# A decoder layer on one core: selective-scan states of two blocks summed on TensorE, the end of softplus on VectorE, feed-forward scales folded into the weights

## The chip, the cores and the metric

The kernel runs on 1 core of one Trainium2 chip. The metric is the device time of one execution in microseconds (us), and the time before is the median of 3 runs. The engines are named PE (TensorE), DVE (VectorE), ACT (ScalarE), POOL (GpSimd) and SP (SyncE, which only issues DMAs here).

## What is computed

One layer over 16 sequences of 64 tokens with 128 features, all in f32: a selective-scan (Mamba) block, a cross-attention without softmax, and a gated feed-forward part, each followed by a layer norm of the sum with its input.

```python
xz = x @ W_in_o + b_in_o
x_proj, z_proj = xz[..., :256], xz[..., 256:]
xm, zm = split(x_proj @ W_in_i)                       # 256 and 256
xc = silu(causal_depthwise_conv(xm, conv_w, conv_b))  # 4 taps
dt, Bm, Cm = split(xc @ W_xp)                         # 128, 16, 16
delta = softplus(dt @ W_dt + b_dt)
h = exp(delta * A) * h + (delta * xc) * Bm            # step by step along the sequence, 16 states per channel
y = sum over states of h * Cm, + D_skip * xc
out = ((y * silu(zm)) @ W_out_i * sigmoid(z_proj)) @ W_out_o + b_out_o
x = layernorm(x + out)
q, k, v = heads of (x, ctx, ctx)                      # 16 heads of 8, q and k of unit length
x = layernorm(x + ((q k^T) ** 2 @ v) @ Wo^T + bo)
h = silu(x @ w1^T * s1) * (x @ w2^T * s2)             # 512 hidden
h = gelu(h @ h1^T * h1s); h = gelu(h @ h2^T * h2s)    # erf gelu
x = layernorm(x + h @ w3^T * s3)
```

## The kernel before

Everything is kept transposed, features on the 128 partitions and tokens along the free axis. The 1024 tokens are cut into 4 blocks of T = 256 (4 sequences). For each block five strands of work are interleaved by hand: front (`xm`, `delta`, `bc`, `soft`, `soft_end`), gates, keys and values, attention with the Mamba output (`mamba_y`, `gate_out`, `proj_out`, then `query`, `attend`, `attn_out`), and feed-forward (`gate_up`, `hid1`, `hid2`, `down`). The table `ORDER` lists for each engine, word by word, in which order it works; the words are executed in that order, so a step that waits holds everything behind it on its engine. `gate_up:1:3` is part 3 of the step for block 1; `scan:9` is scan step 9 of 32.

The scan. The 256 channels are two halves (`CH`), and the 16 states go in 8 steps per block of 2 states (`SG`) each, so one step handles 2 x 2 x 256 = 1024 columns, and the four blocks have 32 steps. A step is four operations on three engines:

- ACT writes the decay exp(delta A) to PSUM (`decay_`, L767, four of 252 columns; `DA_RING` = 2 steps).
- POOL writes the input delta xc B to `state` (`scan_in`, L1054). B and C come broadcast over the partitions through DRAM (`b_fetch`, `c_fetch`, three buffers each).
- DVE runs the recurrence in place (`scan`, L937).
- POOL multiplies the state in place by C (`scan_out`, L1063).

`state` holds two groups of four steps. When the four products of a group are there, DVE sums its 8 states with one reduction (`reduce`, L944) that reads them 512 elements apart, into `part`. PE adds the two parts and D_skip xc (`mamba_y`, L545 and L547), DVE gates the sum (`mamba_y`, L973), PE and DVE go on with `gate_out` (L557, L981).

Softplus (`delta`, `soft`, `soft_end`) is max(p,0) + log(1+exp(-|p|)) with a correction of the rounding: ACT takes Abs (L740), Exp into PSUM (L748) and Ln into SBUF (L752); then DVE takes `trunc` (L918), `rest` (L924) and their sum with the logarithm (L926, its two tensors both in SBUF). The end, delta = pre + rest and du = delta xc (`soft_end_of`, L332 and L336, both inputs in SBUF), is on DVE for block 0 and on POOL for blocks 1 to 3; `scan_in` of the block waits for it. POOL also makes the masked queries (`mask_queries`, L344) for blocks 0 to 2.

The feed-forward part takes the ternary weights as they are. `gate_up` has 4 parts of 128 hidden features: PE (L631), Tanh with the scale on ACT (L834), two operations on DVE (L1023, L1026). `hid1` and `hid2` have 4 parts each: 4 matmuls (L641) and a Gelu of 256 columns with the scale (L842). A layer norm is Square (L790, L786), a matmul with 1/128 (L573), Ln and Exp (L796, L801) and one DVE operation (L1001, L992). ACT's functions need a table to be loaded where they change (L672).

PE's results go through four PSUM banks of 512 columns that are handed out in the order of the list, so a step waits until the fourth result before it has been read. An f32 matmul leaves two matmul records in the trace.

## Time and profile before

| | |
|---|---|
| median of 3 runs (lowest, highest) | 270.6 us (268.74, 270.67) |
| the profiled execution, its own time | 269.1 us |
| its span, first to last instruction | 267.3 us |
| mean granted clock of TensorE | 0.874 of 2.4 GHz |
| busy: PE, DVE, ACT, POOL | 206.5, 184.4, 179.0, 165.4 us |
| table loads on ACT | 41, 52.6 us |

The span is 1.8 us shorter than the execution's own time, and that is 1.5 us under the median. A busy figure is a sum over the whole span; which engine ends a stage is read from the stretches and from what waits. Times within the span are given from its start.

### The profile page before, as it was taken

The page shows a single profiled execution, that of the slowest core. Times are in us where ns is not written, and L with a number is a line of the kernel's source. Part 1 is how long each engine was busy: PE and PEld are TensorE (multiplying, and loading weights), DVE is VectorE, ACT ScalarE, POOL GpSimd, SP SyncE. Part 2 cuts the span into 40 slices and gives each one's busy share as a digit, 9 for nine tenths or more (in the row PEclk, how much of TensorE's full clock was granted, in tenths as well). Part 3 has the DMA queues.
Part 4 walks back from the last instruction along what each step waited for, and adds up shares of the span by engine and source line. Part 5 has one row for each costly group of instructions (what it writes and reads, how often), then busy time and mean ns, then how long its engine had stood idle before and what let it go on. Part 6 is the DMA issues. An engine that isn't in the chain of part 4 may idle for free.

```text
span 267.3 us, 3857 instructions
## 1 busy us (share of the span) xinstructions
PE 206.5 (77%) x1426; PEld 154.3 (58%) x1426; DVE 184.4 (69%) x159; ACT 179.0 (67%) x340; POOL 165.4 (62%) x80
## 2 busy tenths in 40 slices
PE   8996291039585566899949809999999999999992
PEld 6674071017263244686637405777777788778881
DVE  0226619999989998998999998897996452105000
ACT  4055973744898376798976934679966967775523
POOL 4000999999999999999999599599930000000000
PEclk9999777557799555999999855999999999999998
DMA  6986620267105304222046013200000000000000
GB/s 216 422 370 236 237 83 1 78 198 273 75 5 207 114 12 147 81 78 82 0 159 238 2 49 108 81 0 20 4 0 4 20 0 2 2 0 2 21 0 20
DMA packets 6980, 24.38 MB, mean 91 GB/s; under 512 B 945, under 2 KB 1714, under 8 KB 6834
## 3 DMA queue, kind: packets, MB, share of 16 engines
q1 hardware_dynamic: 6962, 24.14, 25.7%
q8 instruction: 11, 0.18, 0.3%
q14 instruction: 7, 0.06, 0.1%
HBM read 23.48 MB, written 0.66 MB: 90 GB/s over the span
## 4 chain that ended last, share of the span: by engine, by line
PE 38%; POOL 22%; DVE 15%; issue 12%; ACT 9%; DMA 2%; SPq 0%; DVEq 0%; ACTq 0%; POOLq 0%
PE work L641 15%; POOL state L1054 11%; POOL state L1063 10%; DVE part L944 10%; PE work L631 4%; ACT L672 3%; DMA cw_row<-cw 2%; PE work L651 2%; DVE state L937 2%; PE work L613 2%; PE work L458 1%; PE work L597 1%; PE work L545 1%; PE work L557 1%; PE work L487 1%
## 5 line engine op out<-in xcount | busy, mean ns | idle before, releaser
L1054 POOL TENSOR_TENSOR state<-du,b_buf 128x1024 f32<-128x1024 f32 x32 | 75.6, 2386 | 26.3 <-DVE du L336 22.9
L1063 POOL TENSOR_TENSOR state<-state,c_buf 128x1024 f32<-128x1024 f32 x32 | 74.7, 2361 | 3.4 <-DVE state L937 3.4
L937 DVE TENSOR_TENSOR_SCAN state<-decay,state 128x1024 f32<-128x1024 f32 x32 | 71.7, 2273 | 5.5 <-ACT decay L767 3.5
L767 ACT ACTIVATE decay<-delta,neg_a 128x252 f32<-128x252 f32 x128 | 52.4, 462 | 19.0 <-DVE state L937 12.4
L944 DVE TENSOR_REDUCE part<-state 128x512 f32<-128x4096 f32 x8 | 58.2, 7289 | 0.2
L672 ACT ACT_TABLE_LOAD x41 | 52.6, 1283 | 1.4 <-PEq L1126 0.7
L641 PE MATMUL work<-hid_b,mat 128*128 128x256 f32 x128 | 29.9, 383 | 0.6 <-ACT zgate L734 0.6
L641 PE MATMUL work<-hid_a,mat 128*128 128x256 f32 x128 | 29.4, 382 | 0.1
L641 PEld LDWEIGHTS work<-hid_b,mat 128*128 128x128 f32 x128 | 23.9, 190 | 5.3 <-ACT zgate L734 1.0
L641 PEld LDWEIGHTS work<-hid_a,mat 128*128 128x128 f32 x128 | 23.9, 190 | 4.5 <-DVE hid_a L1026 0.5
L631 PE MATMUL work<-x,mat 128*128 128x256 f32 x64 | 17.0, 419 | 2.3 <-issue 1.7
L545 PE MATMUL work<-part,mat 128*128 128x512 f32 x16 | 11.0, 825 | 9.3 <-DVE part L944 6.4
L631 PEld LDWEIGHTS work<-x,mat 128*128 128x128 f32 x64 | 12.9, 210 | 6.6 <-issue 4.7
L992 DVE TENSOR_TENSOR final<-work,root_ffn 128x256 f32<-128x256 f32 x4 | 1.7, 418 | 21.8 <-ACT root_ffn L801 21.8
L471 PE MATMUL work<-x,wfz 128*128 128x256 f32 x16 | 5.4, 466 | 14.4 <-DVE vmask L965 13.6
L458 PE MATMUL work<-x,wf 128*128 128x256 f32 (+3 forms) x64 | 15.4, 383 | 0.1
L842 ACT ACTIVATE hid_c<-work,vec 128x256 f32<-128x256 f32 x16 | 7.3, 472 | 10.0 <-PE work L641 9.9
L458 PEld LDWEIGHTS work<-x,wf 128*128 128x128 f32 x64 | 11.7, 191 | 1.8 <-DMA x<-xT 0.5
L471 PEld LDWEIGHTS work<-x,wfz 128*128 128x128 f32 x16 | 3.3, 223 | 15.4 <-DVE vmask L965 13.8
L545 PEld LDWEIGHTS work<-part,mat 128*128 128x128 f32 x16 | 3.8, 256 | 13.2 <-issue 10.1
L1001 DVE SCALAR_TENSOR_TENSOR x<-work,b_centred,root_attn 128x256 f32<-128x256 f32 x8 | 3.8, 480 | 10.7 <-ACT root_attn L801 10.6
L834 ACT ACTIVATE up<-work,half_s 128x256 f32<-128x256 f32 x16 | 7.4, 474 | 5.1 <-PE work L631 3.0
(132 smaller groups left out, 333.5 us busy)
## 6 DMA issues: line engine op xcount, KB each, us to landing
b_buf<-bc_scratch SPq DMA_DIRECT2D x16, 512.0 KB, 3.9
c_buf<-bc_scratch SPq DMA_DIRECT2D x16, 512.0 KB, 4.3
mat<-mats SPq DMA_DIRECT2D x1, 2560.0 KB, 14.6
mat<-mats SPq DMA_DIRECT2D x1, 640.0 KB, 3.9
cw_row<-cw SPq DMA_DIRECT2D x1, 512.0 KB, 6.1
x<-xT SPq DMA_DIRECT2D x1, 512.0 KB, 7.0
kv<-ctxT SPq DMA_DIRECT2D x1, 512.0 KB, 8.9
outT<-final SPq DMA_DIRECT2D x4, 128.0 KB, 1.7
```

The lines of the kernel that those rows point to most:

```text
L458: mm(o[:, :, late:], wf4[:, k, c * P:(c + 1) * P], xs[:, :, 0:SEQ - late], start=(late == 0), stop=False, skip_group_check=True)
L471: i = mm(tile(("zm", b))[:, c * T:(c + 1) * T], wfz[:, c * P:(c + 1) * P], x[:, tok(b)], start=True, stop=True)
L545: mm(o[:, :], ident, part[(GROUPS * b + g) % 2][:, :], start=(g == 0), stop=False, skip_group_check=True)
L631: i = mm(tile(("gu", b, j))[:, n * T:(n + 1) * T], m(w)[:, j * P:(j + 1) * P], x2[b % 2][:, :], start=True, stop=True)
L641: i = mm(tile((key, b, j))[:, 0:T], w[:, k, j * P:(j + 1) * P], src[:, k, :], start=(k == 0), stop=(k == FT - 1))
L672: nc.scalar.preload_act_table_set(name)
L767: i = act_(decay[:, s % DA_RING, k, c, :].rearrange("p (s t) -> p s t", t=SEQ)[:, :, 1:], delta[b % KEEP][:, c, :].rearrange("p (s t) -> p ...
L834: act_(up[j % 2][:, :], tile(("gu", b, j))[:, 0:T], ACT.Tanh, scale=half_s1[:, j:j + 1]).then_inc(up_ready, 1)
L937: vec_.tensor_tensor_scan(h, decay[:, s % DA_RING, :, :, :].rearrange("p k c t -> p (k c t)"), h, 0.0, ALU.mult, ALU.add).then_inc(scanned, 1)
L944: vec_.tensor_reduce(part[g % 2][:, :], state[g % 2][:, :, :, :, :].rearrange("p q k c t -> p (c t) (q k)"), axis=AX.X, op=ALU.add).then_i ...
L1054: nc.gpsimd.tensor_tensor(slot(s), du[b % KEEP][:, None, :, :].broadcast_to([P, SG, CH, T]), b_buf[c % B_RING][:, states, None, :].broadca ...
L1063: nc.gpsimd.tensor_tensor(slot(s), slot(s), c_buf[c % C_RING][:, states, None, :].broadcast_to([P, SG, CH, T]), ALU.mult).then_inc(product, 1)
```

## The change

1. **States.** `state` becomes a ring of 4 steps, and `scan_out` writes its products to a tensor of their own, `prod`. For blocks 0 and 1 PE sums them with the identity into the block's bank, two 512-column matmuls for each step as its product comes (`mamba_sum`, L653 of the changed kernel), and the skip term behind them. For blocks 2 and 3 POOL writes `prod` with the two states of a step side by side, and DVE sums in three reductions: 4 steps, then 3 steps with the first result and the skip term (made by ACT, `skip`), then the last step with the second result; the sum stays in SBUF and DVE gates it from there.
2. **Softplus and masks.** `soft_end` and `mask_queries` are on DVE for all blocks. Exp stays in SBUF, `trunc` and `rest` read it there, and Ln goes to PSUM, beside them. For block 0 the table of Exp and Ln is loaded ahead of `delta`.
3. **Feed-forward.** DVE multiplies the scales into the weights once (`fold`, four operations), and `gate_up`, `hid1` and `hid2` have 2 parts of 512 columns each.
4. **Loads and buffers.** B and C have two buffers each. The weights of the output projection, of the queries and of the feed-forward part are loaded behind the first `bc_store` and, the last 2560 KB, behind `b_fetch:4`, with 1024 KB of broadcast scales. A step that opens a PSUM bank takes the one longest free. Ln and Exp of the norms share a buffer; the bias of the values is one matmul.
5. **Order.** All five lists are written anew.

```diff
-GROUP = 4
-GROUPS = STEPS // GROUP
+GROUP_OF = (0, 0, 0, 0, 1, 1, 1, 2)
+GROUPS = 3
+SLOT_OF = (0, 1, 2, 3, 4, 5, 6, 0)
+SUMMED = (slice(0, 4), slice(4, 8), slice(0, 9, 8))
+EXTRA = (7, 8)
+SLOTS = 9
+SUM_ON = ("pe", "pe", "dve", "dve")
+SOFT_END_ON = ("dve", "dve", "dve", "dve")
+MASK_ON = ("dve", "dve", "dve", "dve")
+OUT_ON_DVE = ()
 TAPS = 4
 HEADS, DK = 16, 8
 HG, HI = 4, 4
...
-B_RING, C_RING = 3, 3
+B_RING, C_RING = 2, 2
+RING = 4
 WARM_UP = 18
-KEEP = 2
+KEEP, XC_KEEP = 2, 3
...
     "dve": """
-        prep prep2 bc:0 delta:0 soft:0 soft_end:0 key_norm:0 scan:0 scan:1 bc:1 delta:1 soft:1 scan:2 scan:3 scan:4
...
+        prep bc:0 delta:0 soft:0 soft_end:0 scan:0 scan:1 scan:2 bc:1 scan:3 prep3 delta:1 soft:1 prep2 scan:4
+        scan:5 soft_end:1 bc:2 delta:2 soft:2 scan:6 scan:7 scan:8 scan:9 key_norm:0 soft_end:2 centre_b fold:0
...
-        state = [sb(f"state{i}", [GROUP, SG, CH, T]) for i in range(2)]
-        part = [sb(f"part{i}", [CH * T]) for i in range(2)]
+        state = [sb(f"state{i}", [SG, CH, T]) for i in range(RING)]
+        prod = sb("prod", [SLOTS, CH, T, SG])
...
-        hid_a, hid_b, hid_c = (sb(n, [FT, T]) for n in ("hid_a", "hid_b", "hid_c"))
+        pre, expo, rest, yg = (sb(n, [CH, T]) for n in ("pre", "expo", "rest", "yg"))
+        hid_a, hid_b = (sb(n, [FT, T]) for n in ("hid_a", "hid_b"))
+        hid_c = hid_a
...
+        def wait_slot_read(eng, s):
+
+            b, n = divmod(s, STEPS)
+            if SUM_ON[b] == "pe":
+                eng.wait_ge(summed, summed_by_pe(s) + 1)
+            else:
+                eng.wait_ge(reduced, reduces_of(b) + GROUP_OF[n] + 1)
...
+        def products(b, n):
+
+            if SUM_ON[b] == "pe":
+                return prod[:, SLOT_OF[n], :, :, :].rearrange("p c t k -> p (c t k)").rearrange("p (k c t) -> p k c t", k=SG, c=CH)
+            return prod[:, SLOT_OF[n], :, :, :].rearrange("p c t k -> p k c t")
...
+        def out_product(eng, engine, s, done):
+
+            c = s // CHUNK
+            b, n = divmod(s, STEPS)
+            slots = [k for k in range(s) if SLOT_OF[k % STEPS] == SLOT_OF[n]]
+            if slots:
+                wait_slot_read(eng, slots[-1])
+            eng.wait_ge(scanned, s + 1)
+            eng.wait_ge(c_loaded[c % C_RING], 16 * (c // C_RING + 1))
+            states = slice(s % CHUNK * SG, (s % CHUNK + 1) * SG)
+            engine.tensor_tensor(products(b, n), slot(s),
+                                 c_buf[c % C_RING][:, states, None, :].broadcast_to([P, SG, CH, T]), ALU.mult).then_inc(done, 1)
...
+            def late(n):
+                if n == 0:
+                    load_mats(4)
+                    load_mats(5)
+                    return
+                load_mats(6)
+                for i, h in enumerate((hid_a, hid_b)):
+                    two = slice(i * 2 * HID, (i + 1) * 2 * HID)
+                    sp.dma_start(h[:, :, :].rearrange("p k t -> p (k t)"), srow[:, two].broadcast_to([P, 2 * HID])).then_inc(loaded["srow"], 16)
...
+            def mamba_sum(s):
+                b, n = divmod(s, STEPS)
+                if SUM_ON[b] == "dve":
+                    return
+                if n == 0:
+                    pe.wait_ge(diag_ready, 1)
+                    wait_bank_free(pe, ("y", b))
+                wait_products(pe, s + 1)
+                for k in range(SG):
+                    i = mm(tile(("y", b))[:, :], ident, products(b, n)[:, k, :, :].rearrange("p c t -> p (c t)"), start=(n == 0 and k == 0),
+                           stop=False, skip_group_check=True)
+                i.then_inc(summed, 1)
...
+                for key, w in (("g", "w1T"), ("u", "w2T")):
+                    wait_bank_free(pe, (key, b, j))
+                    for n in range(2):
+                        i = mm(tile((key, b, j))[:, n * T:(n + 1) * T], m(w)[:, (2 * j + n) * P:(2 * j + n + 1) * P], x2[b % 2][:, :],
+                               start=True, stop=True)
+                    i.then_inc(filled, 1)
...
+                if b == 0:
+                    exp_ln()
...
-                act.wait_ge(soft_dve, b + 1)
-                e = tile(("dl", b))[:, :]
-                act_(e, expo[:, :, :].rearrange("p c t -> p (c t)"), ACT.Exp, scale=-1.0).then_inc(soft_act, 1)
-                if b > 0:
-                    act.wait_ge(soft_rest, 2 * b)
+                act_(expo[:, :, :], expo[:, :, :], ACT.Exp, scale=-1.0).then_inc(soft_act, 1)
                 act.wait_ge(soft_act, 3 * b + 2)
-                act_(logt[:, :, :].rearrange("p c t -> p (c t)"), e, ACT.Ln, bias=1.0).then_inc(soft_act, 1)
+                act.wait_ge(soft_max, b + 1)
...
+            def skip(b):
+
+                if SUM_ON[b] == "pe":
+                    return
+                wait_emptied(act, ("xm", b))
+                if reduces_of(b) > 0:
+                    act.wait_ge(reduced, reduces_of(b) - GROUPS + 2)
+                for c in range(CH):
+                    i = act_(prod[:, EXTRA[0], c, :, 1], xc[b % XC_KEEP][:, c, :], ACT.Copy, scale=v("d_skip")[:, c:c + 1])
+                i.then_inc(skip_ready, 1)
...
+                act_(up[j][:, :, :].rearrange("p n t -> p (n t)"), tile(("g", b, j))[:, :], ACT.Tanh).then_inc(up_ready, 1)
...
-                    act_(dst[:, j, :], tile((key, b, j))[:, 0:T], ACT.Gelu, scale=v(scale)[:, j:j + 1]).then_inc(used["act"], 1)
+                    act_(dst[:, 2 * j:2 * j + 2, :].rearrange("p n t -> p (n t)"), tile((key, b, j))[:, :], ACT.Gelu).then_inc(used["act"], 1)
...
+            def fold(n):
+                dve.wait_ge(loaded["srow"], 32)
+                dve.wait_ge(loaded["w1T"], 16)
+                if n == 0:
+                    vec_.scalar_tensor_tensor(out=m("w1T"), in0=m("w1T"), scalar=0.5, in1=s_row[0], op0=ALU.mult, op1=ALU.mult).then_inc(folded, 1)
+                    vec_.tensor_tensor(m("w2T"), m("w2T"), s_row[1], ALU.mult).then_inc(folded, 1)
+                    return
+                w = m(f"h{n}T").rearrange("p (k n) -> p k n", k=FT)
+                vec_.tensor_tensor(w, w, s_row[n + 1][:, None, :].broadcast_to([P, FT, HID]), ALU.mult).then_inc(folded, 1)
...
             def soft(b):
-                dve.wait_ge(soft_act, 3 * b + 3)
-                e = tile(("dl", b))[:, :].rearrange("p (c t) -> p c t", c=CH)
-                vec_.tensor_scalar(trunc[:, :, :], e, 1.0, -1.0, ALU.add, ALU.add).then_inc(soft_rest, 1)
+                if b > 0:
+                    dve.wait_ge(soft_step, 2 * b - 1)
+                dve.wait_ge(soft_act, 3 * b + 2)
+                vec_.tensor_scalar(rest[:, :, :], expo[:, :, :], 1.0, -1.0, ALU.add, ALU.add).then_inc(soft_rest, 1)
+                dve.wait_ge(soft_rest, 2 * b + 1)
+                vec_.tensor_tensor(rest[:, :, :], expo[:, :, :], rest[:, :, :], ALU.subtract).then_inc(soft_rest, 1)
                 if b == 0:
                     dve.wait_ge(log_one_ready, 1)
-                else:
-                    dve.wait_ge(soft_step, 2 * b - 1)
-                dve.wait_ge(soft_rest, 2 * b + 1)
-                vec_.tensor_tensor(rest[:, :, :], e, trunc[:, :, :], ALU.subtract).then_inc(used["dve"], 1)
-                wait_emptied(dve, ("dl", b))
-                vec_.scalar_tensor_tensor(out=rest[:, :, :], in0=logt[:, :, :], scalar=log_one[:, 0:1], in1=rest[:, :, :],
-                                          op0=ALU.subtract, op1=ALU.add).then_inc(soft_rest, 1)
+                dve.wait_ge(soft_act, 3 * b + 3)
+                dve.wait_ge(soft_rest, 2 * b + 2)
+                log = tile(("dl", b))[:, :].rearrange("p (c t) -> p c t", c=CH)
+                vec_.scalar_tensor_tensor(out=rest[:, :, :], in0=log, scalar=log_one[:, 0:1], in1=rest[:, :, :],
+                                          op0=ALU.subtract, op1=ALU.add).then_inc(used["dve"], 1)
 
             def soft_end(b):
-                if b == 0:
+                if SOFT_END_ON[b] == "dve":
...
-                vec_.tensor_reduce(part[g % 2][:, :], state[g % 2][:, :, :, :, :].rearrange("p q k c t -> p (c t) (q k)"),
-                                   axis=AX.X, op=ALU.add).then_inc(reduced, 1)
+                src = prod[:, SUMMED[n], :, :, :].rearrange("p q c t k -> p (c t) q k")
+                dst = prod[:, EXTRA[n], :, :, 0].rearrange("p c t -> p (c t)") if n < GROUPS - 1 else part
+                vec_.tensor_reduce(dst, src, axis=AX.XY, op=ALU.add).then_inc(reduced, 1)
...
+                dve.wait_ge(reduced, reduces_of(b + 1))
+                vec_.tensor_tensor(yg[:, :, :], part.rearrange("p (c t) -> p c t", c=CH), mgate[b % KEEP][:, :, :],
+                                   ALU.mult).then_inc(y_ready, 1)
...
+                h = hid_a[:, 2 * j:2 * j + 2, :].rearrange("p n t -> p (n t)")
+                dve.wait_ge(up_ready, b * FP + j + 1)
                 if b > 0 and j == 0:
-                    wait_filled(dve, ("h1", b - 1, FT - 1))
-                vec_.scalar_tensor_tensor(out=h, in0=up[j % 2][:, :], scalar=1.0, in1=ps[:, 0:T], op0=ALU.add,
-                                          op1=ALU.mult).then_inc(up_gated, 1)
-                dve.wait_ge(up_gated, n + 1)
-                vec_.scalar_tensor_tensor(out=h, in0=ps[:, T:2 * T], scalar=half_s12[:, j:j + 1], in1=h, op0=ALU.mult,
-                                          op1=ALU.mult).then_inc(used["dve"], 1)
...
+                vec_.scalar_tensor_tensor(out=h, in0=up[j][:, :, :].rearrange("p n t -> p (n t)"), scalar=1.0, in1=tile(("g", b, j))[:, :],
+                                          op0=ALU.add, op1=ALU.mult).then_inc(used["dve"], 1)
+                wait_emptied(dve, ("g", b, j))
+                wait_filled(dve, ("u", b, j))
+                vec_.tensor_tensor(h, tile(("u", b, j))[:, :], h, ALU.mult).then_inc(used["dve"], 1)
```

What the new lists do to the instructions is shown at three places. First DVE, around the start of block 1's scans. Before, `L937` is the scan, `L926` the last of the softplus sums, `L944` the reduction, `L973` and `L981` the gates:

```order
L937 SCALAR_TENSOR_TENSOR state<-decay,state 128x1024 x2
L904 COPY bc_row<-work 32x256
L911 TENSOR_SCALAR pre<-work,vec 128x256 x2
L918 TENSOR_SCALAR trunc<-work 128x512
L924 TENSOR_TENSOR rest<-work,trunc 128x512
L926 SCALAR_TENSOR_TENSOR rest<-logt,log_one,rest 128x512
L937 SCALAR_TENSOR_TENSOR state<-decay,state 128x1024 x6
L965 TENSOR_TENSOR vmask<-work,rk 128x16x8 x2
L944 TENSOR_REDUCE part<-state 128x512 x2
L937 SCALAR_TENSOR_TENSOR state<-decay,state 128x1024 x2
L973 TENSOR_TENSOR yg<-work,mgate 128x512
```

Now, at the same place, `L1091` is the scan, `L406` and `L410` are the end of softplus for block 2, and `L1043`, `L1044` and `L1047` are three of the four folds:

```order
L1091 SCALAR_TENSOR_TENSOR state<-decay,state 128x1024 x4
L1116 TENSOR_SCALAR ssk<-work 128x32
L1119 RECIPROCAL rk<-ssk 128x32
L406 TENSOR_TENSOR delta<-pre,rest 128x512
L410 TENSOR_TENSOR du<-delta,xc 128x512
L1051 COPY b_centred<-work 128x2
L1043 SCALAR_TENSOR_TENSOR mat<-mat,hid_a 128x512
L1044 TENSOR_TENSOR mat<-mat,hid_a 128x512
L1091 SCALAR_TENSOR_TENSOR state<-decay,state 128x1024
L1141 TENSOR_TENSOR yg<-work,mgate 128x512
L1047 TENSOR_TENSOR mat<-mat,hid_b 128x2048
L1155 SCALAR_TENSOR_TENSOR mat<-zgate,work 128x512
```

Two reductions are gone from between the scans of blocks 0 and 1, and five operations with two inputs in SBUF stand there.

Second POOL, at the passage from block 0 to block 1. Before, `L1054` is `scan_in`, `L1063` is `scan_out`, and `L332`, `L336` end the softplus of block 1:

```order
L1054 TENSOR_TENSOR state<-du,b_buf 128x1024 x5
L1063 TENSOR_TENSOR state<-state,c_buf 128x1024 x7
L332 TENSOR_TENSOR delta<-pre,rest 128x512
L336 TENSOR_TENSOR du<-delta,xc 128x512
L1054 TENSOR_TENSOR state<-du,b_buf 128x1024 x4
L1063 TENSOR_TENSOR state<-state,c_buf 128x1024
```

Now `L1228` is `scan_in` and `L429` is `scan_out`:

```order
L1228 TENSOR_TENSOR state<-du,b_buf 128x1024 x2
L429 TENSOR_TENSOR prod<-state,c_buf 128x1024 x4
L1228 TENSOR_TENSOR state<-du,b_buf 128x1024 x4
L429 TENSOR_TENSOR prod<-state,c_buf 128x1024 x2
L1228 TENSOR_TENSOR state<-du,b_buf 128x1024
L429 TENSOR_TENSOR prod<-state,c_buf 128x1024
```

POOL has nothing but the two kinds of scan steps, and it takes them closer together.

Third PE, at the output of block 0. Before, `L545` adds the two parts, `L547` the skip term, and `L557` is `gate_out`:

```order
L471 MATMUL work<-x,wfz 128x256 x2
L478 MATMUL work<-x,mat 128x256 x4
L458 MATMUL work<-x,wf 128x256
...
L545 MATMUL work<-part,mat 128x512 x2
L547 MATMUL work<-xc,diag_d 128x256 x2
L515 MATMUL work<-vec,mat 128x2
L557 MATMUL work<-yg,mat 128x256 x4
```

Now `L653` is the sum of the states (here of steps 5 to 7), `L659` the skip term, `L670` is `gate_out`:

```order
L631 MATMUL work<-mat,k 128x16 x2
L653 MATMUL work<-prod,mat 128x512 x6
L659 MATMUL work<-xc,mat 128x256 x2
L576 MATMUL work<-x,wfz 128x256 x4
L583 MATMUL work<-x,mat 128x256 x4
L670 MATMUL work<-yg,mat 128x256 x4
```

The sum hangs on POOL's product directly, with no step of DVE between.

## Rows read from the trace of the kernel before

**Rows 1.** Stretches of the span: length, busy time (and instructions) by engine, granted clock, DMA.

```profile
core 0: us, PE busy (x) PEld busy (x) DVE busy (x) ACT busy (x) POOL busy (x), PEclk, DMA share, GB/s
0.00:26.20 26.20, 23.41 (x112) 17.45 (x112) 8.23 (x24) 9.59 (x17) 2.75 (x8) 1.00 0.81 310
26.20:145.50 119.30, 75.02 (x419) 52.91 (x420) 107.59 (x69) 87.28 (x176) 118.74 (x53) 0.79 0.35 118
145.50:160.60 15.10, 7.48 (x53) 4.59 (x52) 15.10 (x5) 10.53 (x22) 11.98 (x8) 0.73 0.10 25
160.60:210.30 49.70, 48.89 (x466) 36.62 (x467) 41.29 (x37) 37.44 (x72) 31.96 (x14) 0.95 0.09 31
210.30:267.30 57.00, 51.74 (x379) 42.74 (x378) 12.24 (x28) 34.20 (x57) 0.00 (x0) 0.98 0.02 6
```

**Rows 2.** The chain that ended last, around the first scan step: start, us, what.

```profile
13.62 0.98 PE work L437 x8
...
16.55 0.63 PE work L520 x2
...
19.80 0.94 ACT L672
...
21.73 0.60 ACT logt L752
...
26.17 2.35 POOL state L1054
```

**Rows 3.** Groups by line: busy us, mean ns of one, idle time before and its releasers.

```profile
L1054 POOL TENSOR_TENSOR state<-du,b_buf 128x1024 f32<-128x1024 f32 x32 | 75.6, 2386 | 26.3 <-DVE du L336 22.9 <-DVE part L944 3.3
L937 DVE TENSOR_TENSOR_SCAN state<-decay,state 128x1024 f32<-128x1024 f32 x32 | 71.7, 2273 | 5.5 <-ACT decay L767 3.5 <-POOL state L1054 2.0
L944 DVE TENSOR_REDUCE part<-state 128x512 f32<-128x4096 f32 x8 | 58.2, 7289 | 0.2
L672 ACT ACT_TABLE_LOAD x41 | 52.6, 1283 | 1.4 <-PEq L1126 0.7
L834 ACT ACTIVATE up<-work,half_s 128x256 f32<-128x256 f32 x16 | 7.4, 474 | 5.1 <-PE work L631 3.0 <-DVE hid_a L1023 2.1
L344 POOL TENSOR_TENSOR qmask<-q,vec 128x1024 f32<-128x1024 f32 x3 | 6.0, 2016 | 0.2 <-ACT q L807 0.2
L336 POOL TENSOR_TENSOR du<-delta,xc 128x512 f32<-128x512 f32 x3 | 3.8, 1280 | 0.2
L748 ACT ACTIVATE work<-expo 128x512 f32<-128x512 f32 x4 | 2.4, 596 | 1.8 <-DVE pre L911 1.8
L344 DVE TENSOR_TENSOR qmask<-q,vec 128x1024 f32<-128x1024 f32 x1 | 1.2, 1226 | 3.0 <-ACT q L807 3.0
L336 DVE TENSOR_TENSOR du<-delta,xc 128x512 f32<-128x512 f32 x1 | 0.7, 693 | 0.0
```

**Rows 4.** DVE in order of time: start, us, engine, line; the four times of L926.

```profile
23.88 0.75 DVE L926 SCALAR_TENSOR_TENSOR rest<-logt,log_one,rest 128x512 f32<-128x512 f32 x1
...
41.65 1.26 DVE L926 SCALAR_TENSOR_TENSOR rest<-logt,log_one,rest 128x512 f32<-128x512 f32 x1
...
89.82 1.98 DVE L926 SCALAR_TENSOR_TENSOR rest<-logt,log_one,rest 128x512 f32<-128x512 f32 x1
...
139.57 6.55 DVE L926 SCALAR_TENSOR_TENSOR rest<-logt,log_one,rest 128x512 f32<-128x512 f32 x1
```

**Rows 5.** POOL in order of time, beside the waits of rows 4 and steady.

```profile
42.32 2.79 POOL L1054 TENSOR_TENSOR state<-du,b_buf 128x1024 f32<-128x1024 f32 x1
...
91.22 2.81 POOL L1054 TENSOR_TENSOR state<-du,b_buf 128x1024 f32<-128x1024 f32 x1
...
133.96 11.62 POOL L1063 TENSOR_TENSOR state<-state,c_buf 128x1024 f32<-128x1024 f32 x5
```

**Rows 6.** PE in order of time: `gate_out:3`, and the sixteen matmuls of `hid2:3`.

```profile
210.33 1.89 PE L557 MATMUL work<-yg,mat 128*128 128x256 f32 x8
...
252.74 7.07 PE L641 MATMUL work<-hid_b,mat 128*128 128x256 f32 x32
```

403 lines of the change are left out of this document (233 added, 170 removed).

## The prediction

> **What bounds the kernel now.** I read the stretches first [rows 1], cut where the scan phase changes hands: from POOL's first scan step (26.2 us) to the last product of block 2 (145.5), from there to the moment PE can take that block's output (160.6), from there to `gate_out` of block 3 (210.3), and the tail. In the first, POOL is busy 118.7 of 119.3 us and DVE 107.6: the scan runs at POOL's pace, with DVE 90% full beside it. In the second DVE is busy all the time (two reductions) and PE half. In the third and fourth PE is busy 48.9 of 49.7 and 51.7 of 57.0, at a clock near 2.4 GHz; POOL works 32 of the 49.7 us and not at all after them, so it does not decide there. So the end is the sum of four things: POOL's start, POOL's 48 operations for blocks 0 to 2 with what it does between, 15 us of reductions, and 107 us of PE.
>
> The chain at the start [rows 2] shows what precedes POOL: the bias matmuls of `prep2` (0.98 us), the keys of block 0 (0.63), a table load that shows for 0.94, Ln (0.60). The groups [rows 3] give prices. Last, L926, the one DVE operation that reads two tensors in SBUF while POOL works: 0.75 us with POOL idle, and 1.26, 1.98 and 6.55 with POOL busy [rows 4]. In the first two cases DVE got in where one POOL operation followed another, and that next one took 2.79 and 2.81 us instead of the 2.32 of its neighbours (11.62 for five) [rows 5]. In the third it was passed over at two such places. So these operations exclude POOL's, and the wait is a POOL operation's remainder or more.
>
> The Trainium skill, page "SBUF — State Buffer", section "Who interferes with whom", says why: a VectorE operation with two SBUF inputs takes the port pair that GpSimd reads through, whole instructions at a time. Rows 4 agree, and add that the lock can be lost twice running.
>
> **Start.** Removed from the chain are the four pieces of rows 2, 0.98 + 0.63 + 0.94 + 0.60 = 3.2 us (Ln now lies beside `trunc` and `rest`; the table is loaded under the delta matmuls). POOL starts at 23.0. `b_fetch:0` now has 768 KB of weights ahead of it on SP's queue but the 2560 KB no longer; I take it as landed, and 2 us late as the bound.
>
> **POOL.** The 64 scan operations stay, at a pitch of 2.32 [rows 5]: 48 take 111.4 us, 16 take 37.1. Three ends of softplus (2 x 1.28 each) and three masks (2.02) go [rows 3], 13.7 us. Products into a tensor of their own, from block 2 with a step of 8 bytes in the output, are not in the trace; the bounds are no change (input and output in place take the same 2.3 us) and 10% on 16 products, 4 us. I take no change.
>
> **The port.** What leaves POOL comes to DVE with two SBUF inputs, and the change adds more of these: for blocks 1 to 3 the subtraction in `soft` (3) and `soft_end` (6), masks 0 to 2 (3), the folds (4), the gate of block 2 (1): 17 while POOL works, where there were 3. L926 itself now reads PSUM and leaves the list. A wait was 0.5, 1.2 and 5.8 us (rows 4 less 0.75), median 1.2, mean 2.5. I take 1.9, between them: 32 us on DVE. POOL loses 0.45 for each short one [rows 5], about 1.0 for a mask and 2 for a large fold, 12 us in all. So POOL gains 13.7 and pays 12: alone it would bring block 2's last product at 23.0 + 111.4 + 11 = 145.4, as before.
>
> By the same page (section "Who interferes with whom") also single-source f32 operations from SBUF to SBUF contend; that would be `trunc` of blocks 1 to 3 and three small ones, six more waits, some 11 us by 1.9 each. No row shows such an operation beside POOL, so the sum leaves it out.
>
> **DVE up to block 2's gate.** In the first stretch DVE was busy 107.6 us [rows 1]. Four reductions go (4 x 7.3 = 29.2), and L926 with its waits (1.26 + 1.98 + 5.9 of the last one = 9.2); 69.2 stay, 24 scans at 2.2 [rows 3] among them. To these come L926 at its bare 0.75 three times (2.3); the ends of softplus, 6 x 0.69 (4.2); two masks (2.5); the folds, 0.7 + 0.7 + 2.3 + 2.3 (512 elements take 0.69 and 1024 take 1.23 [rows 3], 1.05 ns for an element more); gate, values and diagonal that now fall here (2.0); and three reductions. 4096 elements read 512 apart cost 7.29 us [rows 3], 1.78 ns each. Now two neighbours lie together. Bounds: 4.4 us as if contiguous, 7.3 as before. I take 5.0, nearer the contiguous row since half of the jumps go, and 2.6 for the short one, 12.6 together. The pairs in `gate_up` save 0.8. Sum: 69.2 + 2.3 + 4.2 + 2.5 + 6.0 + 2.0 + 12.6 - 0.8 = 98.0. DVE stood 11.7 us in that stretch [rows 1], for decays and POOL; I keep half, 5.5. It starts at 25.3, one POOL operation after 23.0. With 15 waits of 1.9 (28.5) block 2 is gated at 25.3 + 98.0 + 5.5 + 28.5 = 157.3. POOL would allow 145.4 + 2.6 + 0.7 = 148.7: DVE is the bound.
>
> The page's section "Door 1: The DMA port swizzle" says that two accesses to one 16-byte line hide the jump. Then the reductions cost 4.4, and the sum falls by 2 us; the trace has no row of it.
>
> **DVE to block 3's gate.** 8 scans (17.6), reductions 5.0 + 5.0 + 2.6, `gate_up` 2.8, mask 1.2, the rest 4.5, one wait 1.9: 40.6. `gate_out:3` can start at 197.9. POOL's 16 operations from 145.4 end by 185, and PE's work from `gate_out:2` to `gate_out:3` is 72 matmuls of 256 columns at 0.43 (16 in 6.9 us [rows 6]) and 3.5 us of attention, 34.5: 157.3 + 34.5 = 192. Neither decides, each has 6 us or more of room.
>
> **What is hidden.** The state sums add 32 matmuls of 512 columns (27.8 us) and take away eight and four short ones, 19 us net, in the stretch where PE was busy 75 of 119 at 0.79 of the clock. They are short and each step's two follow a product; at 1.2 GHz they take 3.5 us per 4.7 us of POOL's time. Cover gone, block 1's attention is late and `gate_out:2` with it: up to 5 us. POOL needs a sum only when it comes round to the slot (after the eighth step). ACT loses ten table loads (41 to 31, 12.8 us) and about 8 us by 512-column functions (0.60 against 2 x 0.47); it had 32 us free in that stretch, so nothing shows. The 3.6 MB behind `b_fetch:4` stand before `c_fetch:3`: at most 4 us, once, taken as 0.
>
> **Tail.** After `gate_out:3` the same 57.0 us of work stand [rows 1, 6], with one norm matmul more (0.4). The paired parts cost in front of `hid1:3`: Tanh and Gelu of 512 columns are 0.12 later each, and hid1 starts when two DVE operations of 0.69 instead of 0.45 are done; `down:2` is now ahead of the last `gate_up` and no longer covers it. By these rows PE stands 1.1 us more. 57.0 + 0.4 + 1.1 = 58.5.
>
> **Sum.** 197.9 + 58.5 = 256.4 is the span, and 1.8 more the own time: 258.2. The profiled execution is 1.5 under the median of the runs, so the forecast is 259.7, taken as 260.0 (3.9% less than 270.6).
>
> **Rivals.**
> - *DVE gets in at every boundary.* For it: two of three rows. Each wait is then 1.2 or less, DVE gains 16 x 0.7 = 11, and POOL decides: last product at 185, the two last reductions and the gate done at 191, and 58.5 + 3.3: 253. If the port costs POOL nothing either, PE is next: 148.7 + 34.5 + 58.5 + 3.3 = 245. Chance 0.20.
> - *Reductions as slow as before.* 2.3 us more on each of four and 1.1 on two, all on DVE's path: 11 more, 271. For it: nothing in the trace shows a faster one. Chance 0.12.
> - *The port takes what POOL gave.* The mean wait is that of the rows, 2.5, or the single-source ones wait too (the page's rule above): 17 x 0.6 or 11 us more, 270. Against it: a POOL that waits for scans leaves the port free. Chance 0.12.
> - *Slower.* The wait of row 139.57 is the rule where POOL has a row of ready products: 5.8 for 1.9. Its place is the subtraction and the two ends of softplus, on which `scan_in` of the next block waits. Each costs 3.9; four of them make the change worth nothing beyond 273, six give 283. Chance 0.11.
> - *Forecast*, DVE bound with some of each: 254 to 267. Chance 0.45.
>
> A measurement of this kernel can tell about 1% from no change: under 267.9 is faster, over 273.3 slower. Faster: 0.45 + 0.20 and a fifth of the two cases at 270, 0.70. Slower: 0.11 and an eighth of those two, 0.14. The rest, 0.16, is within 1%. The range, 246 to 274, runs from PE as the bound to the two cases at 270 with their upper edge, and leaves out the slow rival.
>
> **What would show it.** Right: the two-input DVE operations (L406, L410, L437, L1074, the folds) at a mean of 2 to 3 us each where POOL is busy; POOL idle 10 us or more for scans; the reduction near 5 us; POOL's first step at 23; the table group at 31; PE's sums never ahead of POOL in what a wait names; 58 us from `gate_out:3` to the end. Wrong: POOL without idle time (then the first rival), L1108 at 7 us (the second), any single L406 or L410 over 5 us again and again (the fourth), or PE as what DVE and POOL wait for.

## The result and the profile after

The changed kernel takes 262.26 us (median of 4 runs, 261.55 to 264.52) against 269.67 of the kernel before beside it: ratio 0.974, 95% interval 0.969 to 0.979. The forecast was 260.0 us, a ratio of 0.961 against its 270.6. So 2.6% was gained where 3.9% was forecast. In the profiled execution the span fell from 267.3 to 260.4 us, 6.9 less, and the own time is 262.3.

| Point in the span | before | forecast | after |
|---|---|---|---|
| first scan step on POOL | 26.2 | 23.0 | 23.0 |
| gate of block 2 begins (before: its sum can be taken) | 160.6 | 156.6 | 155.9 |
| gate of block 2 done | | 157.3 | 156.8 |
| last product on POOL done | 196.1 | about 185 | 192.9 |
| `gate_out:3` begins on PE | 210.3 | 197.9 | 199.6 |
| from there to the end | 57.0 | 58.5 | 60.8 |
| span | 267.3 | 256.4 | 260.4 |

The stretches of the span after the change, cut where the forecast cut them (stretch and length, then busy time and count by engine, granted clock, DMA share), against [rows 1]:

```profile
core 0: us, PE busy (x) PEld busy (x) DVE busy (x) ACT busy (x) POOL busy (x), PEclk, DMA share, GB/s
23.00:156.00 133.00, 108.02 (x539) 68.93 (x538) 121.89 (x84) 89.38 (x185) 124.21 (x50) 0.88 0.37 131
156.00:199.60 43.60, 40.12 (x445) 31.34 (x443) 40.12 (x33) 36.76 (x69) 33.27 (x15) 1.00 0.17 53
199.60:260.40 60.80, 53.41 (x379) 42.02 (x378) 10.68 (x20) 24.86 (x41) 0.00 (x0) 0.98 0.02 8
```

Up to block 2's gate DVE is busy 121.9 of 133.0 us and POOL 124.2: neither is full, and each stands for the other at times. PE has 108 us there, where before it had 75 of 119, at a granted clock of 0.88 instead of 0.79. The stretch of 15 us that two reductions on DVE filled from end to end [rows 1] is gone.

The groups of DVE between 20 and 215 us (busy us, mean ns of one, idle before and who ended it), where the forecast had its prices:

```profile
L1091 DVE TENSOR_TENSOR_SCAN state<-decay,state 128x1024 f32<-128x1024 f32 x32 | 72.1, 2276 | 6.4 <-POOL state L1228 4.5 <-ACT decay L897 1.9
L1108 DVE TENSOR_REDUCE prod<-prod 128x512 f32<-128x4096 f32 x4 | 17.6, 4412 | 2.0 <-POOL prod L429 2.0
L437 DVE TENSOR_TENSOR qmask<-q,vec 128x1024 f32<-128x1024 f32 x4 | 13.3, 3334 | 0.0
L1074 DVE TENSOR_TENSOR rest<-expo,rest 128x512 f32<-128x512 f32 x3 | 8.2, 2722 | 0.1
L410 DVE TENSOR_TENSOR du<-delta,xc 128x512 f32<-128x512 f32 x4 | 6.8, 1708 | 0.1
L406 DVE TENSOR_TENSOR delta<-pre,rest 128x512 f32<-128x512 f32 x4 | 6.2, 1560 | 0.0
L1047 DVE TENSOR_TENSOR mat<-mat,hid_b 128x2048 f32<-128x2048 f32 x2 | 5.3, 2636 | 0.0
L1108 DVE TENSOR_REDUCE mat<-prod 128x512 f32<-128x2048 f32 x2 | 4.6, 2281 | 0.1
L1072 DVE TENSOR_SCALAR rest<-expo 128x512 f32<-128x512 f32 x3 | 4.5, 1497 | 0.0
```

The scan costs what it did (2273 ns [rows 3]). A reduction of 4096 elements takes 4.41 us where 7.29 was the price of before [rows 3]. The masks (L437) average 3.33 us against a bare 1.23 [rows 3], the subtraction (L1074) 2.72. `trunc` (L1072), one input and one output in SBUF, took 0.42 us while POOL had not begun and 1.5 on average of the three beside it. The first two of its rows:

```profile
18.51 0.42 DVE L1072 TENSOR_SCALAR rest<-expo 128x512 f32<-128x512 f32 x1
...
39.97 1.79 DVE L1072 TENSOR_SCALAR rest<-expo 128x512 f32<-128x512 f32 x1
```

POOL in order of time: the rows that have a wait of 1 us or more in front of them.

```profile
23.00 9.28 POOL L1228 TENSOR_TENSOR state<-du,b_buf 128x1024 f32<-128x1024 f32 x4 [19.74 <-DMA b_buf<-bc_scratch]
49.09 5.11 POOL L429 TENSOR_TENSOR prod<-state,c_buf 128x1024 f32<-128x1024 f32 x2 [2.36 <-DVE state L1091]
...
74.44 2.35 POOL L429 TENSOR_TENSOR prod<-state,c_buf 128x1024 f32<-128x1024 f32 x1 [3.02 <-PE work L653]
...
149.25 2.38 POOL L429 TENSOR_TENSOR prod<-state,c_buf 128x1024 f32<-128x1024 f32 x1 [3.42 <-issue]
...
188.21 4.69 POOL L429 TENSOR_TENSOR prod<-state,c_buf 128x1024 f32<-128x1024 f32 x2 [3.41 <-DVE state L1091]
```

The four stalls behind the first row, with one of 0.21 us that is not shown, are the 12.4 us that POOL loses between 23 and 193. The second is a wait for PE: step 8's product goes where step 0 and step 7 lay, and their sum came late. The one at 149 us, for which the profile names nobody, ends as DVE finishes the scan that stood behind a mask of 5.30 us.

### The profile page after: what moved, and what is told of

Same layout as the page of the kernel before. It is cut to its first block, busy times and chain, and to the rows that moved or that the text cites. A ratio compares the mean times of both kernels' runs of the same rounds, so it can differ in the third digit from the quotient of the medians.

```text
span 260.4 us, 3882 instructions
## 1 busy us (share of the span) xinstructions
PE 223.2 (86%) x1458; PEld 158.4 (61%) x1458; DVE 180.0 (69%) x153; ACT 160.3 (62%) x310; POOL 160.2 (62%) x71
## 4 chain that ended last, share of the span: by engine, by line
PE 33%; DVE 22%; issue 17%; POOL 14%; ACT 7%; DMA 5%; SPq 0%; DVEq 0%; POOLq 0%; ACTq 0%
PE work L760 13%; DVE state L1091 8%; POOL prod L429 7%; POOL state L1228 7%; PE work L563 4%; ACT L792 3%; DVE qmask L437 3%; DMA b_buf<-bc_scratch 2%; DVE rest L1074 2%; DMA cw_row<-cw 2%; PE work L653 2%; DVE prod L1108 2%; PE work L710 2%; PE work L686 2%; PE work L670 1%
## 5 line engine op out<-in xcount | busy, mean ns | idle before, releaser
L1228 POOL TENSOR_TENSOR state<-du,b_buf 128x1024 f32<-128x1024 f32 x32 | 82.1, 2586 | 19.7 <-DMA b_buf<-bc_scratch 19.7
L429 POOL TENSOR_TENSOR prod<-state,c_buf 128x1024 f32<-128x1024 f32 x32 | 76.4, 2407 | 12.4 <-DVE state L1091 6.0
L1091 DVE TENSOR_TENSOR_SCAN state<-decay,state 128x1024 f32<-128x1024 f32 x32 | 72.1, 2276 | 6.4 <-POOL state L1228 4.5
L653 PE MATMUL work<-prod,mat 128*128 128x512 f32 x64 | 35.0, 691 | 10.3 <-DVE mat L1032 7.8
L792 ACT ACT_TABLE_LOAD x31 | 39.8, 1283 | 1.3 <-PEq L1296 0.7
L653 PEld LDWEIGHTS work<-prod,mat 128*128 128x128 f32 x64 | 13.5, 220 | 25.5 <-issue 12.3
L1108 DVE TENSOR_REDUCE prod<-prod 128x512 f32<-128x4096 f32 x4 | 17.6, 4412 | 2.0 <-POOL prod L429 2.0
L563 PE MATMUL work<-x,wf 128*128 128x256 f32 (+3 forms) x64 | 17.9, 428 | 0.2 <-DVE bf L1015 0.2
L984 ACT ACTIVATE hid_a<-work 128x512 f32<-128x512 f32 x8 | 4.8, 597 | 14.5 <-PE work L760 14.5
L437 DVE TENSOR_TENSOR qmask<-q,vec 128x1024 f32<-128x1024 f32 x4 | 13.3, 3334 | 0.0
L710 PE MATMUL work<-qmask,keys 32*64 32x256 f32 x128 | 8.8, 389 | 3.5 <-DVE qmask L437 2.4
L984 ACT ACTIVATE hid_b<-work 128x512 f32<-128x512 f32 x8 | 4.8, 596 | 11.4 <-PE work L760 11.4
## 6 DMA issues: line engine op xcount, KB each, us to landing
mat<-mats SPq DMA_DIRECT2D x1, 2560.0 KB, 10.5
```

The source lines that it names most:

```text
L429: engine.tensor_tensor(products(b, n), slot(s), c_buf[c % C_RING][:, states, None, :].broadcast_to([P, SG, CH, T]), ALU.mult).then_inc(don ...
L437: engine.tensor_tensor(qmask[:, :, :], q[:, None, :].broadcast_to([P, HI, T]), v("hmask")[:, :, None].broadcast_to([P, HI, T]), ALU.mult). ...
L563: mm(o[:, :, late:], wf4[:, k, c * P:(c + 1) * P], xs[:, :, 0:SEQ - late], start=(late == 0), stop=False, skip_group_check=True)
L653: i = mm(tile(("y", b))[:, :], ident, products(b, n)[:, k, :, :].rearrange("p c t -> p (c t)"), start=(n == 0 and k == 0), stop=False, ski ...
L710: i = mm(tile(("s", b, g))[e * SEQ:(e + 1) * SEQ, p * HI * SEQ:(p + 1) * HI * SEQ], keysT[b % KEEP][r, t:t + SEQ], qmask[r, :, t:t + SEQ], ...
L792: nc.scalar.preload_act_table_set(name)
```

## The experiments

Ratios are to the kernel before, run beside it on the same chip; "gate 2" and "gate 3" are the starts of `mamba_y:2` and `mamba_y:3` on DVE in the profiled execution. The first column of times is the span of that execution. The executions of one kernel lie 1 to 4.2 us apart, and not all rows come from one chip. So a difference of spans or gates is one pair of executions, and it is the ratios that decide.

| Kernel | span | gate 2 | gate 3 | median us | ratio (95%) |
|---|---|---|---|---|---|
| changed kernel | 260.4 | 155.9 | 197.7 | 262.26 | 0.974 (0.969 to 0.979) |
| e1 reductions read 512 apart | 272.1 | 161.6 | 208.0 | 272.98 | 1.013 (1.008 to 1.018) |
| e2 masks from PSUM | 257.5 | 151.6 | 194.8 | 258.81 | 0.960 (0.954 to 0.966) |
| e3 end of softplus on POOL, late | 273.2 | 168.8 | 210.6 | 274.57 | 1.018 (1.011 to 1.024) |
| e4 no folding | 256.5 | 150.6 | 193.9 | 257.74 | 0.951 (0.943 to 0.958) |
| e5 block 2 summed on PE | 267.6 | 160.4 | 205.0 | 269.64 | 1.001 (0.999 to 1.004) |
| e6 all sums on DVE | 279.9 | 174.0 | 217.2 | 281.69 | 1.045 (1.039 to 1.051) |
| e7 end of softplus on POOL, early | 265.9 | 160.0 | 203.2 | 267.05 | 0.989 (0.983 to 0.996) |
| e8 the end | 259.5 | 155.3 | 198.5 | 261.99 | 0.970 (0.964 to 0.977) |
| e9 three moves of order | 267.3 | 159.9 | 204.7 | 267.58 | 0.987 (0.981 to 0.993) |
| e10 e2, e8 and e9 | 260.8 | 159.0 | 199.8 | 262.38 | 0.970 (0.964 to 0.976) |
| e11 e10, sums 14 and 15 ahead | 262.6 | 159.0 | 201.6 | 265.32 | 0.980 (0.975 to 0.985) |
| e12 e2 and e8 | 255.1 | 152.1 | 194.1 | 255.94 | 0.947 (0.940 to 0.953) |

The theory at the start was that of the forecast: DVE sets the pace up to block 3's gate, slowed by waits for a port that it shares with POOL. The rival was that POOL, or PE with its sums, is as near to the path as DVE.

**e1: the layout of the products.** The two states of a step 512 elements apart again.

```diff
-            if SUM_ON[b] == "pe":
-                return prod[:, SLOT_OF[n], :, :, :].rearrange("p c t k -> p (c t k)").rearrange("p (k c t) -> p k c t", k=SG, c=CH)
-            return prod[:, SLOT_OF[n], :, :, :].rearrange("p c t k -> p k c t")
+            return prod[:, SLOT_OF[n], :, :, :].rearrange("p c t k -> p (c t k)").rearrange("p (k c t) -> p k c t", k=SG, c=CH)
...
-                src = prod[:, SUMMED[n], :, :, :].rearrange("p q c t k -> p (c t) q k")
+                src = prod[:, SUMMED[n], :, :, :].rearrange("p q c t k -> p q (c t k)").rearrange("p q (k n) -> p n q k", k=SG)
```

> One part undone: POOL writes the products of blocks 2 and 3 as it does those of blocks 0 and 1, the two states of a step 512 elements apart, and the three reductions of each block read them 512 apart. Theory A (VectorE sets the pace up to the gate of block 3, and the neighbours of 8 bytes are what makes a reduction cheap): the 4096-element reductions take 7.3 us again instead of 4.4 and the 2048-element ones 3.6 instead of 2.3, 2 x (2.9 + 2.9 + 1.3) = 14 us more on VectorE, all on the path: 276 us, slower than the kernel before. Rival B (VectorE has slack before both gates, since it also waits for GpSimd and TensorE there): half of that is hidden, 269 us. Rival C (the layout is not what counts, the reductions in three pieces are): 4.4 us stay and the time is 262 us.

The one line of the reduction in this kernel (count, then shortest, median and longest in ns, first and last start):

```profile
L1109 DVE TENSOR_REDUCE prod<-prod x4: 7204/7325/7397, 134.7 to 196.6; 128x512 f32<-128x4096 f32 x4
L1109 DVE TENSOR_REDUCE mat<-prod x2: 3699/3745/3791, 157.6 to 204.2; 128x512 f32<-128x2048 f32 x2
```

A reduction costs 1.8 ns an element when its two neighbours are 512 apart and 1.08 when they lie together. Six reductions are 14.6 us longer in sum, gate 3 is 10.3 later and the span 11.7 longer: 0.7 of the added time counts at the gate and 0.8 in the span, between A and B and nearer to A, and C is out. The 1.4 us between the two lie behind gate 3, where the edit changes nothing; why was not looked for. With this one part undone the kernel is 1.3% slower than before. The other side of the layout cost nothing: POOL's undisturbed products take 2.35 us in both kernels, with a step of 8 bytes in the output or without.

**e2: one SBUF operand less in the masks.**

```diff
-            engine.tensor_tensor(qmask[:, :, :], q[:, None, :].broadcast_to([P, HI, T]), v("hmask")[:, :, None].broadcast_to([P, HI, T]),
-                                 ALU.mult).then_inc(qm_ready, 1)
+            engine.scalar_tensor_tensor(out=qmask[:, :, :], in0=tile(("q", b))[:, None, 0:T].broadcast_to([P, HI, T]), scalar=v("bq"),
+                                        in1=v("hmask")[:, :, None].broadcast_to([P, HI, T]), op0=ALU.add, op1=ALU.mult).then_inc(used["dve"], 1)
...
-                act_(q[:, :], tile(("q", b))[:, 0:T], ACT.Identity, bias=v("bq")).then_inc(q_ready, 1)
```

> One cost taken away: the masked queries are made from PSUM, (q + bias) x mask in one VectorE operation with one large SBUF operand less, and ScalarE's copy of q falls away. Theory A (port): masks 0, 1 and 2 take 1.2 us each beside a busy GpSimd instead of 3.4, 5.3 and 3.4; VectorE gains 8.4 us before the gate of block 3 and the time falls by 7 to 8 us, to 254 us. Rival B (VectorE is not alone on the path; GpSimd's own stalls and TensorE's queue take over): masks 1.2 us but a gain of only 2 to 4 us, 259 us. Rival C (the long durations are a wait for something else than the SBUF port): masks stay at 3 us or more and the time at 262 us.

The group of the masks in this kernel, and that of the two large folds:

```profile
L1044 DVE TENSOR_TENSOR mat<-mat,hid_b 128x2048 f32<-128x2048 f32 x2 | 6.8, 3416 | 0.0
...
L437 DVE SCALAR_TENSOR_TENSOR qmask<-work,vec 128x1024 f32<-128x1024 f32 x4 | 5.1, 1271 | 0.0
```

The masks cost 1.27 us whether POOL works or not, so the long durations hung on where the input lies: C is out. The masks save 8.2 us, the span falls by 2.9 and the median by 3.5, which is B's range. Part of the rest is seen in the first row: others wait more, the large folds at 3.42 instead of 2.64 us, and one of the small ones at 2.84 instead of 0.68. In sum the two-input operations other than the masks wait 3.8 us more than in the changed kernel.

**e3 and e7: the end of softplus back on POOL.** e3 has it late in POOL's list, e7 where DVE's list has it.

```diff
-SOFT_END_ON = ("dve", "dve", "dve", "dve")
+SOFT_END_ON = ("dve", "pool", "pool", "pool")
```

> One part undone: the end of softplus of blocks 1 to 3 is on GpSimd again, ahead of steps 8, 15 and 22 of scan_in. VectorE loses six operations that took 11.7 us with their waits, GpSimd gets 3 x 2 x 1.28 = 7.7 us. Theory A (VectorE alone sets the pace): about 10 us less, 252 us. Rival B (GpSimd has 12 us of idle time before its last product and about as much stretched operations, so what it takes over is paid from there and the trade is even): 260 to 264 us. Rival C (what GpSimd gave up was the gain of the change): slower, 268 us or more.

What DVE waited for in e3 (us in total, times, the longest), the row of interest:

```profile
DVE pre L1065 <- POOL delta L407: 20.4, 2, 12.3
```

DVE stood 12.3 us in one piece: `delta:3` on DVE may overwrite `pre` only when POOL has read it, and POOL came to that step only at 102 us. So e3 measured a bad place in the list and says nothing on the trade, though its time falls under C.

> The end of softplus of blocks 1 to 3 on GpSimd as in e3, but at the places in its list that answer to those of VectorE's list: ahead of steps 6, 10 and 18 of scan_in. In e3 VectorE stood 12.3 us in one piece for the end of block 2's softplus, which came late in GpSimd's list. Theory A (that wait was all that made e3 slow; the trade itself is even, since what GpSimd gets, 7.7 us, is about 0.65 of the 11.7 us that VectorE loses): 260 to 264 us. Rival B (GpSimd's time is dearer than VectorE's, because every scan step passes through it): 267 us or more. Rival C (VectorE's is dearer): 258 us or less.

In e7, DVE between 23 and 205 us:

```profile
DVE state L1092 <- POOL state L1229: 10.3, 5, 3.5
DVE mat L1190 <- PE work L727: 6.1, 1, 6.1
DVE pre L1065 <- POOL delta L407: 3.5, 1, 3.5
```

In the changed kernel the first of these is 4.5 us and the second 1.1. DVE was relieved of 11.7 us and gave 14.3 of them back in waits for POOL's inputs, POOL's `delta` and block 0's attention (5.8 + 3.5 + 5.0); the last product ends 5.5 us later and so does the span. It is 267.05 us, at the edge of B: against these places in POOL's list, moving the work to DVE was worth 4 to 5.5 us although DVE takes 1.5 times as long over it. So POOL's time was the dearer one here. As e3 shows how much the place matters, a better one could still change that; no other was tried.

**e4: the folding left out.** The words `fold:0` to `fold:2` are taken out of DVE's list, and what waited for them waits for the loads.

> One cost taken away: the four operations that multiply the scales of the feed-forward part into its weights are left out, so this kernel computes without those scales; the loads stay. VectorE has 6.6 us less to do between 60 and 110 us. Theory A (each microsecond of VectorE before the gate of block 3 counts): 6.6 us less, 255.7 us. Rival B (what VectorE gains there it loses again in waits for GpSimd and TensorE): 1 to 3 us less, 260 us.

6.6 us less on DVE moved gate 3 by 3.8 and the span by 3.9 us; the two ratios with their intervals allow 3 to 10 us. The time lies between A and B. By the gates 0.6 of DVE's time counts, less than in e1 and more than in e2, where 2.9 of 8.2 us did; the intervals are too wide to order e4 and e2. The scales cost what DVE pays for them; what it would cost to have them in the 256-column functions as before was not tried.

**e5 and e6: who sums.** e5 lets PE sum block 2 too; e6 gives all sums to DVE.

```diff
-SUM_ON = ("pe", "pe", "dve", "dve")
+SUM_ON = ("pe", "pe", "pe", "dve")
...
-SUM_ON = ("pe", "pe", "dve", "dve")
+SUM_ON = ("dve", "dve", "dve", "dve")
```

The first pair of lines is e5's, the second e6's.

In e5 the words `mamba_sum:16` to `mamba_sum:23` stand between `hid1:0:0` and `hid2:0:1` in PE's list and three reductions are gone from DVE's; in e6 six are added, and `skip:0`, `skip:1` on ACT.

> The change's own idea taken one block further: block 2's states too are summed by TensorE with the identity, 16 matmuls of 512 columns (14 us at 2.4 GHz) laid between the attention and feed-forward steps of block 1, and VectorE loses three reductions, 11.1 us. Theory A (VectorE sets the pace up to both gates; the runs with the scales and the masks taken away gave back about 0.65 of what VectorE lost): 7 us less than the changed kernel, 255 us. Rival B (from 116 us on TensorE is about as full as VectorE, so its sums come late and hold both GpSimd's slots and block 2's gate): 262 us or more, and GpSimd waits for the sums by more than the 3 us it does now.

In e5 the stretch up to gate 2:

```profile
116.00:160.40 44.40, 41.79 (x181) 27.81 (x180) 22.69 (x20) 30.55 (x55) 41.86 (x17) 1.00 0.29 107
```

DVE is busy half of it and PE 41.8 of 44.4 us at the full granted clock. The gate waits 14.15 us for PE's last sum and comes 4.5 us later than with DVE summing. The two last products were ready when PE was at `hid2:0` and the attention. Rival B holds, with its mechanism on the gate and not on POOL's slots: POOL's wait for PE stayed at 3.1 us.

> The sums of TensorE taken back: the states of blocks 0 and 1 are reduced on VectorE as those of blocks 2 and 3 are, in the new layout with neighbours of 8 bytes; the skip terms come from ScalarE. VectorE gets six reductions, 22.2 us; TensorE loses 36 matmuls. Theory A (the gain of the sums on TensorE is VectorE's time, at about 0.7 of it): 15 us more, 277 us, slower than the kernel before. Rival B (TensorE's sums cost something too: GpSimd's wait of 3 us for a slot and the late attention of block 1 go with them): 6 to 9 us more, 270 us.

In e6, what POOL waited for, over the whole span:

```profile
POOL prod L427 <- DVE mat L1106: 18.6, 2, 11.3
POOL prod L427 <- DVE state L1089: 10.1, 4, 3.7
```

22.2 us of reductions on DVE made the span 19.5 us longer, more than the 15 of A. Twice, at the start of blocks 1 and 2, POOL stands for the slots that a reduction behind scans and gates must free first. The sums on PE are thus the largest of the parts that were undone here: by themselves worth more than the whole gain. The stretch from 23 to 156 us in e6:

```profile
23.00:156.00 133.00, 73.70 (x378) 50.61 (x376) 127.10 (x81) 76.56 (x164) 107.76 (x44) 0.68 0.32 117
```

PE is busy 73.7 us in it at a granted clock of 0.68, and 108.0 at 0.88 in the changed kernel. From gate 3 to the end both take 62.7 us, so the sums left no debt on PE behind them.

**e8: the end.** `hid2` of blocks 2 and 3 writes to a state buffer, and PE's list has `norm_var:3:2 hid2:2:1 gate_up:3:0 gate_up:3:1 down:2 hid1:3:0 norm_var:2:3`.

```diff
-        hid_c = hid_a
+        hid_c = [hid_a[:, :, :]] * 2 + [state[0].rearrange("p g c t -> p (g c t)").rearrange("p (k t) -> p k t", k=FT)] * 2
```

> The end alone: the output of hid2 for blocks 2 and 3 goes to a state buffer that is free by then, so that gate_up of block 3 needs no longer wait for down of block 2; on TensorE norm_var:3:2 stands before hid2:2:1, gate_up:3 before down:2, and norm_var:2:3 behind hid1:3:0. Theory A (the tail is 2.2 us longer than predicted because nothing covers tanh and the two gating operations of block 3): 1 to 2 us less, 260.5 us, and less idle time ahead of hid1 of block 3. Rival B (the gaps move, a table load more shows on ScalarE): 262 to 264 us.

PE around the feed-forward part of block 3 in the changed kernel:

```profile
233.17 0.70 PE L686 MATMUL work<-sq_ffn,mat 128*128 128x256 f32 x2 [0.85 <-DVE x L1175]
233.71 3.75 PE L745 MATMUL work<-x,mat 128*128 128x256 f32 x16
238.39 7.54 PE L760 MATMUL work<-hid_a,mat 128*128 128x256 f32 x32 [0.93 <-DVE hid_a L1201]
```

and in e8:

```profile
231.70 3.62 PE L743 MATMUL work<-x,mat 128*128 128x256 f32 x16
235.15 0.59 PE L765 MATMUL work<-x,mat 128*128 128x256 f32 x2
235.58 1.89 PE L769 MATMUL work<-state,w_c 128*128 128x256 f32 x8
237.31 3.62 PE L758 MATMUL work<-hid_a,mat 128*128 128x256 f32 x16
```

Both gaps are closed, and from gate 3 to the end it takes 61.0 us instead of 62.7, as theory A has it. That this is no scatter is seen over the kernels: the four that have this end (e8, e10, e11, e12) all take 61.0 us there, and the others but e1 62.6 or 62.7. The whole time is within its scatter of the changed kernel's, since gate 3 came 0.8 us later in this execution.

**e9: three moves of order.**

```diff
-        delta:2 mamba_sum:2 mamba_sum:3 mamba_sum:4 centre_w centre_b xm:3 key_norm:0 mamba_sum:5 mamba_sum:6
+        delta:2 mamba_sum:2 mamba_sum:3 mamba_sum:4 centre_w mamba_sum:5 centre_b xm:3 key_norm:0 mamba_sum:6
...
-        prep bc_store:0 late:0 b_fetch:0 b_fetch:1 c_fetch:0 c_fetch:1 b_fetch:2 b_fetch:3 bc_store:1 c_fetch:2
+        prep bc_store:0 b_fetch:0 b_fetch:1 late:0 c_fetch:0 c_fetch:1 b_fetch:2 b_fetch:3 bc_store:1 c_fetch:2
```

and `prep2` right behind `prep` on DVE.

> Three moves of order, nothing else: late:0 (768 KB of weights) goes behind b_fetch:1 on the queue of SyncE; the product of step 5 is summed by TensorE ahead of centre_b, where it stood 4.7 us with the product lying ready; prep2 on VectorE (one multiplication of 128 x 128, 1.52 us beside GpSimd) is done before GpSimd starts. Theory A (GpSimd's first step waited about 1 us for a fetch that had the weights ahead of it, and its stall of 3.0 us at 74.4 us is 1.8 us of TensorE's sum of step 5): the first step at 22.1 us, the stall about 1.2 us, and by 0.65 of what is gained before the gates some 2 us less than the changed kernel, 260 us. Rival B (the first step hangs on softplus and not on the fetch; the stall moves to the next slot): 262 us.

Both causes were right, and the kernel became slower: 6.9 us by the span, which is that of its slowest execution, 5.3 by the medians and 3.5 by the ratios. POOL starts at 22.10 and waits there for DVE, no more for the fetch; its stall at 74 us is gone. What it brought DVE, in order of time, in the changed kernel:

```profile
69.98 2.00 DVE L406 TENSOR_TENSOR delta<-pre,rest 128x512 f32<-128x512 f32 x1
72.01 0.69 DVE L410 TENSOR_TENSOR du<-delta,xc 128x512 f32<-128x512 f32 x1
...
72.69 0.68 DVE L1043 SCALAR_TENSOR_TENSOR mat<-mat,hid_a 128x512 f32<-128x512 f32 x1
73.29 0.68 DVE L1044 TENSOR_TENSOR mat<-mat,hid_a 128x512 f32<-128x512 f32 x1
...
76.67 2.28 DVE L1047 TENSOR_TENSOR mat<-mat,hid_b 128x2048 f32<-128x2048 f32 x1
```

and in e9:

```profile
70.15 2.01 DVE L405 TENSOR_TENSOR delta<-pre,rest 128x512 f32<-128x512 f32 x1
72.20 2.72 DVE L409 TENSOR_TENSOR du<-delta,xc 128x512 f32<-128x512 f32 x1
...
74.91 2.76 DVE L1042 SCALAR_TENSOR_TENSOR mat<-mat,hid_a 128x512 f32<-128x512 f32 x1
77.59 2.83 DVE L1043 TENSOR_TENSOR mat<-mat,hid_a 128x512 f32<-128x512 f32 x1
...
83.13 4.12 DVE L1046 TENSOR_TENSOR mat<-mat,hid_b 128x2048 f32<-128x2048 f32 x1
```

The same five operations cost 14.4 us instead of 6.3. From 71.4 to 74.4 us POOL had stood, and three operations with two SBUF inputs passed at their bare price in it. Over the whole scan phase the seventeen such operations have 31.2 us of waits in e9 and 23.0 in the changed kernel. DVE's lateness then comes back to POOL:

```profile
91.92 2.36 POOL L428 TENSOR_TENSOR prod<-state,c_buf 128x1024 f32<-128x1024 f32 x1 [6.82 <-issue]
```

it waits 6.8 us for the scan behind them. So neither A nor B: DVE had used the stall, and to take its 3.0 us away cost 3.5 to 7 us. The other runs bear this out. The five operations take 6.3 to 6.4 us where POOL stood 3.0 or 3.1 us (changed kernel, e5), 8.3 and 8.4 where it stood 2.6 and 2.8 (e12, e8), 10.2 where it stood 1.7 (e2), and 14.4 where it did not stand (e9, e10).

**e10, e11 and e12: together.**

> The masks from PSUM (e2), the end (e8) and the three moves of e9 together. Theory A (the three act at different places and add: 3.5, 1.7 and 2 us): 255 us. Rival B (what is gained on VectorE is lost to GpSimd and TensorE before the gate of block 3): as e2 alone, 258 to 259 us.

> As e10, and on TensorE the sum of step 14 stands ahead of attend_out:0 and that of step 15 ahead of attn_out:0. In e2 GpSimd stood 2.5 us at 119 us for the slot that step 15's sum still had to read. Theory A (GpSimd's time counts before block 2's gate as VectorE's does): 1 to 2 us less than e10, 253 to 254 us. Rival B (the sums now hold attn_out:0, and with it gate_up:0 and what follows on ScalarE): no less than e10.

> The two parts that helped or did no harm, without the moves of e9: the masks from PSUM (e2) and the end (e8). Theory A (they act in different stretches and add, and what made e10 slow were e9's moves, which took from VectorE the time in which GpSimd stood and the port was free): 257 us, 1.5 to 2 us less than e2, with the folds and the end of block 2's softplus at about 0.7 us each again. Rival B (the end's gain is not real beyond the scatter of runs): as e2, 258.8 us. Rival C (e10's loss came from combining the masks with the end): 262 us.

e10 is 262.38 us, worse than e2 alone and so neither A nor B. DVE shows e9's durations again at that place (2.71, 2.76, 2.83 and 4.12 us). e12, which is e10 without e9's three moves, is 255.94 us, as its theory A had it: the moves cost 6 us here too. In e11 the sum of step 15 came earlier and POOL's stall of 5.01 us at 126 us fell to 0.60; the kernel became 2.9 us slower, rival B by its number; whether by the mechanism that B names was not taken apart. e12 shows the cheap passage again:

```profile
72.65 0.69 DVE L408 TENSOR_TENSOR du<-delta,xc 128x512 f32<-128x512 f32 x1
...
73.33 0.68 DVE L1038 SCALAR_TENSOR_TENSOR mat<-mat,hid_a 128x512 f32<-128x512 f32 x1
73.93 0.68 DVE L1039 TENSOR_TENSOR mat<-mat,hid_a 128x512 f32<-128x512 f32 x1
```

beside a stall of POOL of 2.61 us; only the large fold behind them takes 4.18 us. e12 beats both kernels: 0.947 of the time before (0.940 to 0.953), 2.8% below the changed kernel, 6 to 7 us. The three moves of e9 were not run one by one; the rows put the harm on the sum of step 5, since the stall was a wait for PE's sums, but this is argued and not shown.

## Why the forecast came out right, and where its terms were off

The main mechanism held: DVE, lengthened by its waits beside POOL, reached the gates within 1 us of the forecast, and PE followed. The closeness of the whole is in part luck. The span was forecast 4.0 us short (256.4 for 260.4), the median only 2.3: the forecast had added 1.5 us because the profiled execution of the kernel before lay that far under its median, and this time it lay at the median. The 4.0 are -0.5 at block 2's gate, 1.0 to block 3's, 1.2 of waiting for PE, and 2.3 in the tail.

- **The start** was right to 0.1 us, by luck of two terms. Softplus was done at 22.0, and POOL then waited 1 us for `b_fetch:0` behind 768 KB of weights, which the forecast took as landed (with 2 us as the bound); e9 has the step at 22.10 without them.
- **The reductions** were mis-sized: 5.0 and 2.6 us taken, 4.41 and 2.28 measured. The lower bound, as if contiguous, was what came. By the Trainium skill ("SBUF — State Buffer", "Door 1: The DMA port swizzle", two accesses to one line hide the jump) the forecast's side sentence had 4.4; the trace agrees. That e1 is 11.7 us longer is the rival "reductions as slow as before" (11 us) as it would have been.
- **The port.** The seventeen two-input operations wait 23.0 us in sum, 1.35 each, where 1.9 was taken. But the six single-source operations that the sum left out do contend: `trunc` three times, the two multiplications for the diagonal and the one in `prep2` lose 7.2 us. 30.2 us against a term of 32: the total was right since one error covered the other. That was luck, and the rival "the port takes what POOL gave" had this one of its conditions right, with 7.2 us for its 11. By the Trainium skill ("SBUF — State Buffer", "Who interferes with whom") they contend; the rows of `trunc` agree, 0.42 us before POOL starts and 1.24 to 1.79 beside it, and it should have gone into the sum. The mean of 1.35 is that of this order: it holds waits from 0 to 4.1 us, and it was low since some operations fell into POOL's stalls, as e9 shows (31.2 us for the same seventeen).
- **DVE as the bound** was too simple a step. The gate of block 2 was done at 156.8 for 157.3, by two errors: from its first scan at 25.4 DVE was busy 122.7 us for the 126.5 of the sum, and stood 8.7 us for POOL, ACT and PE where 5.5 was kept. Taking 6.6 to 8 us from DVE gave 2.9 to 3.9, adding 14.6 cost 11.7 and adding 22.2 cost 19.5 (e4, e2, e1, e6), and giving POOL 7.7 us more while DVE had 11.7 less cost 5.5 (e7). Both engines, and the hand-overs between them, set the pace.
- **The sums on PE hidden** was right as to PE's own time, and it held as long as two blocks were summed: e5 shows the cover gone with the third. What was missed is the 3.0 us that POOL stood for a slot at 74 us, against the sign that the forecast had named ("PE's sums never ahead of POOL"); the text had looked only at the sums' length, not at the softplus of block 2 for which PE stood 4.7 us ahead of them.
- **From gate to gate.** 40.6 us were taken for the 41.6 from the end of gate 2 to the end of gate 3. Then `gate_out:3` waited for PE, which was at `down:1`: y was ready at 198.4 and PE at 199.6, where the forecast had left PE 6 us of room. POOL's last product came at 192.9, 8 us later than the forecast's 185; 6 of these were there at block 2 (151.6 for 145.4). Its 48 steps were busy 119.8 us for the 122.4 taken, and the stalls at 49, 74 and 149 us, 8.8 together, had no term in POOL's sum, though the signs asked for a POOL that stands 10 us. With two reductions behind it, it was nearer to the path than the forecast had it.
- **The tail** was mis-sized, 58.5 for 60.8. PE stands 2.1 us more than before (7.4 idle of 60.8 against 5.3 of 57.0), where 1.1 was taken. Its busy time is 1.7 us longer over as many matmul records (379), where only the 0.4 of the added norm matmul was taken; the rest is not explained here. e8 takes 1.7 us off the end, 1.2 of them idle time of PE and 0.5 busy, so the buffer and the order around `gate_up:3` were a cause of it; they were moved together.
- **ACT** lost its ten table loads (31 at 1283 ns) and nothing of it shows, as taken.
- **The late weights** were taken as 0 with 4 us as the bound, for which no working was given: the 2560 KB took 10.5 us from issue to landing. The 0 held, since POOL waits for a load only before its first step.

Of the rivals, "DVE gets in at every boundary" would have been refuted by the masks at 5.30 us and the subtraction at 2.72 each time; "slower" by the absence of a wait of 5 us on the operations that it named (the longest of them takes 2.73 us).

## What to carry to other kernels

When two engines share a port by turns, the price of an operation depends on what the other does at that moment: make its operand come from PSUM (1.27 us for 3.33) before moving it about, and look at what passes through an engine's stall before removing the stall. Before giving an idle engine more work, look at what stands ahead of it in that engine's order: the sums cost little on TensorE for two blocks (one stall of GpSimd, 3.0 us) and the third took the whole gain. And the place of a step in an in-order list can weigh more than which engine has it: e3 and e7 differ by 7 us in three words.

## What was not expected of the hardware

- In these runs TensorE's granted clock was higher where it was given more work: with the sums of blocks 0 and 1 on it the granted clock between 23 and 156 us was 0.88 with 108 us busy, without them 0.68 with 74 us busy (e6), and in e5 it was 1.00 from 116 to 160 us with 41.8 of 44.4 us busy. 1.00 is the upper of the two levels, 2.4 GHz.
- Small operations waited as long beside POOL as large ones. The multiplication of 128 x 128 in `prep2`, one input in SBUF, took 0.29 us at 10.5 us in e9, before POOL had begun, and 1.52 at 45.3 us in the changed kernel; two of that size for the diagonal took 3.22 beside POOL there and 4.61 in e9.
- A VectorE operation that waits for the port comes out at nearly the same time again and again: the subtraction in `soft` took 2.71 to 2.73 us at each of its three places in the changed kernel and in e1, e2, e3, e4 and e7. It follows `trunc`, which itself had to wait for the port; that it therefore always meets a step of POOL that has just begun is how these rows read, and was not tested by itself.
